# Storing the results of the mixture-of-experts units in order of the units, and gathering them by places that VectorE works out once per expert stage

## The reference, cut to what matters

```python
router_probs = jax.nn.softmax(flat @ router_w + router_b)
topk_probs, topk_idx = jax.lax.top_k(router_probs, 2)            # 2 of 8 experts for each of 4096 tokens
sh = jax.nn.gelu(flat @ sw1 + sb1); shared_out = sh @ sw2 + sb2  # 256 -> 512 -> 256, for every token
h1 = jax.nn.gelu(jnp.einsum('td,edh->teh', flat, rw1) + rb1)
expert_out = jnp.einsum('teh,ehd->ted', h1, rw2) + rb2
out = shared_out + sum of topk_probs * expert_out of the two chosen experts
```

## Time and profile before

| | |
|---|---|
| median of 3 runs | 4138.96 us (4134.91 to 4142.33) |
| the profiled execution, from its first to its last instruction (span) | 4122.5 us |
| median less span | 16.5 us |
| busy: PE, DVE, ACT, POOL | 3626.3, 2877.5, 1924.7, 1607.9 us |
| mean granted clock of PE | 0.951 of full speed |
| moved by DMA | 358.33 MB, of which 74.4 MB are the 142 clears of 512 KB |

### The profile page before, as it was taken

How to read it: one execution, slowest core, us unless ns; L and a number is a source line. 1 busy time by engine, 2 the same in 40 slices (tenths; PEclk the granted TensorE clock), 3 DMA queues, 4 the chain that set the end, 5 groups by cost and what they waited for, 6 DMA issues and landing times. The chain is left out here.

```text
span 4122.5 us, 60134 instructions
## 1 busy us (share of the span) xinstructions
PE 3626.3 (88%) x19193; PEld 2601.5 (63%) x19256; DVE 2877.5 (70%) x5355; ACT 1924.7 (47%) x4079; POOL 1607.9 (39%) x1485
## 2 busy tenths in 40 slices
PE   4888877999599999998799869887899799999998
PEld 3555556888588888887788735444666455554666
DVE  5777656656566666645665568886888666776898
ACT  3565644344355555544344344443344465666332
POOL 3766726444465666633644321101002444441000
PEclk8999978999899999999899989999999999999999
DMA  5999902465100000001356410001201444441000
GB/s 135 302 259 269 307 23 84 151 194 162 59 16 19 19 19 19 16 4 35 100 167 180 148 48 21 21 11 23 40 0 39 91 101 109 102 114 27 11 16 16
DMA packets 228873, 358.33 MB, mean 87 GB/s; under 512 B 36482, under 2 KB 132850, under 8 KB 221810
## 3 DMA queue, kind: packets, MB, share of 16 engines
q1 hardware_dynamic: 204038, 265.38, 22.1%
q0 software_dynamic: 24544, 89.36, 8.9%
HBM read 173.82 MB, written 172.20 MB: 84 GB/s over the span
## 5 line engine op out<-in xcount | busy, mean ns | idle before, releaser
L2894 DVE TENSOR_REDUCE ab_nmx<-banks 128x1 f32<-128x512 f32 x512 | 329.0, 684 | 136.0 <-PE banks L2681 133.8
L2825 ACT ACTIVATE ab_pt<-banks 128x512 f32<-128x512 f32 x512 | 283.0, 600 | 163.9 <-PE banks L2691 154.9
L1736 POOL TENSOR_TENSOR lb_pq<-lb_pq,lb_rr 128x512 f32<-128x512 f32 x192 | 206.2, 1077 | 305.1 <-DVE lb_rr L1597 301.8
L1462 ACT ACTIVATE lb_pq<-banks,lb_nmx 128x256 f32<-128x256 f32 x384 | 178.5, 470 | 229.4 <-DVE lb_nmx L1592 226.2
L2691 PE MATMUL banks<-ab_qT,ab_kT 128*128 128x512 f32 x512 | 252.3, 497 | 5.7 <-ACT ab_pt L2825 5.7
L358 ACT ACTIVATE da_pt<-banks 128x512 f32<-128x512 f32 (+1 forms) x384 | 179.3, 537 | 124.9 <-PE banks L270 120.6
L1592 DVE TENSOR_REDUCE lb_nmx<-banks 128x2 f32<-128x512 f32 x192 | 131.1, 683 | 148.0 <-PE banks L1314 146.8
L2681 PE MATMUL banks<-ab_kT,ab_qT 128*128 128x512 f32 x512 | 208.1, 410 | 21.1 <-DVE ab_nmx L2894 14.6
L285 PE MATMUL banks<-da_pt,da_vx 128*64 128x512 f32 (+3 forms) x1024 | 165.0, 467 | 35.3 <-POOL da_pt L578 31.8
L2465 PE MATMUL banks<-w_f_dT,f_hT 128*128 128x256 f32 x768 | 178.1, 382 | 4.0 <-ACT f_hT L2511 4.0
L576 POOL TENSOR_TENSOR da_pt<-da_pt,w_da_tri 128x384 f32<-128x384 f32 x128 | 148.0, 1157 | 85.7 <-ACT da_pt L358 85.6
(11 more groups left out here) (538 smaller groups left out, 11146.5 us busy)
## 6 DMA issues: line engine op xcount, KB each, us to landing
moe_xs<-zero SPq DMA_DIRECT2D x71, 512.0 KB, 11.8
moe_ys<-zero SPq DMA_DIRECT2D x71, 512.0 KB, 11.8
moe_a_w_raw<-in_moe_w SPq DMA_DIRECT2D x48, 512.0 KB, 3.9
moe_b_w_raw<-in_moe_w SPq DMA_DIRECT2D x48, 512.0 KB, 4.0
da_spill<-da_hi SPq DMA_DIRECT2D x128, 128.0 KB, 2.4
ab_spill<-ab_hi SPq DMA_DIRECT2D x128, 128.0 KB, 2.4
ab_qT<-ab_spill POOLq DMA_DIRECT2D x32, 392.0 KB, 5.7
ab_kT<-ab_spill POOLq DMA_DIRECT2D x32, 392.0 KB, 5.3
```

The source lines that it names most:

```text
L1462: nc.scalar.activation(pq[:, n % RING, t, :], ps[:, S_BANK + n % 2, 2 * P * t:2 * P * t + 2 * P], ACT.Exp, bias=nmx[:, n % RING, t:t + 1], ...
L1736: nc.gpsimd.tensor_tensor(pq[:, n % RING, :, :], pq[:, n % RING, :, :], bcast(rr[:, n % RING, :], 2, 2 * P), ALU.mult).then_inc(s_p, 1)
L2825: nc.scalar.activation(pt[:, s % RING, :], ps[:, EXP_BANK + s % 3, :], ACT.Exp, scale=AB_D ** -0.5).then_inc(s_e, 1)
L2894: nc.vector.tensor_reduce(nmx[:, g % 2, col:col + 1], ps[:, MAX_BANK + n % 3, :], op=ALU.max, axis=AX.X, negate=True).then_inc(s_mx, 1)
```

## The change

`store_y` writes unit u's result to rows 512u to 512u + 511 of `moe_ys`, a fixed address, and `moe_ys` shrinks to 23 x 512 = 11776 rows. It is no longer cleared: `clear_regions` runs over `moe_xs` alone (71 clears, 10 or 11 in a batch). The scatter still goes by `place` as before, and units still load their tokens and weights by the table. Since results now stand elsewhere than tokens, DVE rewrites `place` once per expert stage, in a new job `result_places` in step i = N - UNITS - 1 = 9, between `low_x(11)` and `take(9)`: to each place it adds, for the expert chosen, (first unit of the expert x 512 - its region). For that the places and the chosen experts are kept as floats for all batches in `Choice` (`placef`, `chosen_by`), and the counts and ends of the experts are worked out on 128 partitions, not one: the matmul of totals gives 128 rows, and `moe_fill` and `moe_upto` are loaded as broadcasts to 128 partitions.

```diff
@@ class Choice
+        self.placef = space.enter_context(core.nc.sbuf_tensor(f"{tag}_placef", [P, B, NT, TOPK], F32))
+        self.chosen_by = space.enter_context(core.nc.sbuf_tensor(f"{tag}_chosen_by", [P, B, NT, TOPK], F32))
@@ experts
-        count, ends, tablei = sb("count", [1, NE]), sb("ends", [1, NE]), sb("tablei", [1, 2, UNITS], U32)
+        count, ends, tablei = sb("count", [P, NE]), sb("ends", [P, NE]), sb("tablei", [1, 2, UNITS], U32)
...
+        taken = y[:, 0:2, :].rearrange("p t c -> p (t c)").rearrange("p (n e) -> p n e", e=NE)
@@ store_y
-                    sp.dma_start(rows_of(ys, entry(1, u, ROWS - UNIT)), y[:, :, :]).then_inc(s_stored[u % 2], 16)
+                    sp.dma_start(ys[u * UNIT:(u + 1) * UNIT, :].rearrange("(t p) c -> p t c", p=P),
+                                 y[:, :, :]).then_inc(s_stored[u % 2], 16)
@@ ranks
-                        nc.tensor.matmul(ps[0:1, ROUTE_BANK, 0:NE], w["moe_ones"][:, 0:1], before[:, NT, :],
+                        nc.tensor.matmul(ps[:, ROUTE_BANK, 0:NE], w["moe_ones"][:, :], before[:, NT, :],
@@ DVE, new job
+                def result_places():
+                    nc.vector.tensor_tensor(base[:, :], ends[:, :], count[:, :], ALU.subtract)
+                    dve.drain()
+                    nc.vector.scalar_tensor_tensor(base[:, :], base[:, :], float(UNIT), w["moe_region"][:, :],
+                                                   ALU.mult, ALU.subtract)
+                    experts_of = idf[:, :, :, :].rearrange("p b t k -> p (b t k)")
+                    rows = placef[:, :, :, :].rearrange("p b t k -> p (b t k)")
+                    nc.vector.tensor_tensor(taken[:, :, :], bcast(w["moe_iota"][:, :], 1, B * NT * TOPK),
+                                            bcast(experts_of, 2, NE), ALU.is_equal)
+                    dve.drain()
+                    nc.vector.tensor_tensor(taken[:, :, :], taken[:, :, :], bcast(base[:, :], 1, B * NT * TOPK), ALU.mult)
+                    dve.drain()
+                    nc.vector.reduce_sum(experts_of, taken[:, :, :], axis=AX.X)
+                    dve.drain()
+                    nc.vector.tensor_tensor(rows, rows, experts_of, ALU.add)
+                    dve.drain()
+                    for k in range(2):
+                        dve.wait_ge(s_scatter[k], per_batch * B // 2)
+                    nc.vector.tensor_copy(place[:, :, :, :].rearrange("p b t k -> p (b t k)"), rows)
+                    dve.drain()
@@ DVE, the loop over items
                     if i + 2 in number:
                         low_x(i + 2)
+                    if i == N - UNITS - 1:
+                        result_places()
                     if i in number:
                         take(i)
@@ network
-            ("moe_fill", a["moe_fill"]), ("moe_upto", a["moe_upto"]), ("moe_unit", a["moe_unit"])])
+            ("moe_fill", a["moe_fill"][0].partition_broadcast(P)), ("moe_upto", a["moe_upto"][0].partition_broadcast(P)),
+            ("moe_unit", a["moe_unit"])])
-        w["moe_ys"] = nc.dram_tensor("moe_ys", (ROWS, C), F32).ap()
+        w["moe_ys"] = nc.dram_tensor("moe_ys", (UNITS * UNIT, C), F32).ap()
@@ clear_regions
-            for k in range(part * 2 * blocks // parts, (part + 1) * 2 * blocks // parts):
-                rows = (w["moe_xs"], w["moe_ys"])[k // blocks][k % blocks * UNIT:(k % blocks + 1) * UNIT, :]
+            for k in range(part * blocks // parts, (part + 1) * blocks // parts):
+                rows = w["moe_xs"][k * UNIT:(k + 1) * UNIT, :]
```

More of the change, by code:

```diff
@@ L697, in experts @@
         top, idx = sb("top", [P, NT, 8]), sb("idx", [P, NT, 8], U32)
-        idf = sb("idf", [P, NT, TOPK])
-        tw, place = choice.tw, choice.place
+        tw, place, placef, idf = choice.tw, choice.place, choice.placef, choice.chosen_by
         oh = [sb(f"oh{k}", [P, NT, NE]) for k in range(TOPK)]
@@ L702, in experts @@
         b2 = sb("b2", [P, 2, C])
-        placef = sb("placef", [P, NT, TOPK])
+        base = sb("base", [P, NE])
         rank, spot = sb("rank", [P, NT, NE]), sb("spot", [P, TOPK, NT, NE])
-        count, ends, tablei = sb("count", [1, NE]), sb("ends", [1, NE]), sb("tablei", [1, 2, UNITS], U32)
+        count, ends, tablei = sb("count", [P, NE]), sb("ends", [P, NE]), sb("tablei", [1, 2, UNITS], U32)
         shift = sb("shift", [P, B, NT])
@@ L984, in weights @@
                     dve.drain()
-                    nc.vector.tensor_copy(idf[:, :, :], idx[:, :, 0:TOPK])
+                    nc.vector.tensor_copy(idf[:, b, :, :], idx[:, :, 0:TOPK])
                     dve.drain()
@@ L988, in weights @@
                         nc.vector.tensor_tensor(oh[k][:, :, :], bcast(w["moe_iota"][:, :], 1, NT),
-                                                bcast(idf[:, :, k], 2, NE), ALU.is_equal)
+                                                bcast(idf[:, b, :, k], 2, NE), ALU.is_equal)
                     dve.drain()
@@ L1008, in places @@
                     for k in range(TOPK):
-                        nc.vector.reduce_sum(placef[:, :, k], spot[:, k, :, :], axis=AX.X)
+                        nc.vector.reduce_sum(placef[:, b, :, k], spot[:, k, :, :], axis=AX.X)
                     dve.drain()
-                    nc.vector.tensor_copy(place[:, b, :, :], placef[:, :, :])
+                    nc.vector.tensor_copy(place[:, b, :, :], placef[:, b, :, :])
                     dve.drain().then_inc(s_place, 1)
@@ L1015, in units @@
                     dve.wait_ge(s_total, 1)
-                    nc.vector.tensor_copy(count[:, :], ps[0:1, ROUTE_BANK, 0:NE])
+                    nc.vector.tensor_copy(count[:, :], ps[:, ROUTE_BANK, 0:NE])
                     dve.drain()
                     nc.vector.tensor_tensor(parts_of[:, :, :], bcast(count[:, :], 2, NE),
-                                            bcast(w["moe_fill"][0:1, :], 1, NE), ALU.is_gt)
+                                            bcast(w["moe_fill"][:, :], 1, NE), ALU.is_gt)
                     dve.drain()
@@ L1022, in units @@
                     dve.drain()
-                    nc.vector.tensor_tensor(parts_of[:, :, :], bcast(count[:, :], 1, NE), w["moe_upto"][0:1, :, :], ALU.mult)
+                    nc.vector.tensor_tensor(parts_of[:, :, :], bcast(count[:, :], 1, NE), w["moe_upto"][:, :, :], ALU.mult)
                     dve.drain()
@@ L1026, in units @@
                     dve.drain()
-                    nc.vector.tensor_tensor(passed[:, :, :], bcast(w["moe_unit"][0:1, :], 2, NE), bcast(ends[:, :], 1, UNITS),
+                    nc.vector.tensor_tensor(passed[:, :, :], bcast(w["moe_unit"][0:1, :], 2, NE), bcast(ends[0:1, :], 1, UNITS),
                                             ALU.is_ge)
@@ L1031, in units @@
                     dve.drain()
-                    nc.vector.tensor_tensor(passed[:, :, :], passed[:, :, :], bcast(count[:, :], 1, UNITS), ALU.mult)
+                    nc.vector.tensor_tensor(passed[:, :, :], passed[:, :, :], bcast(count[0:1, :], 1, UNITS), ALU.mult)
                     dve.drain()
@@ L3270, in _ @@
             def _(sp):
-                sp.wait_ge(s_clear, 16 * 2 * ROWS // UNIT)
+                sp.wait_ge(s_clear, 16 * ROWS // UNIT)
         early.close()
```

2 lines of the change are left out of this document (1 added, 1 removed).

## The result

| | before | changed |
|---|---|---|
| median | 4136.24 us of 20 runs (4130.05 to 4146.87) | 4144.56 us of 20 runs (4134.63 to 4153.63) |
| ratio, 95% interval | 1 | 1.0018 (1.0010 to 1.0027) |
| the profiled execution, span | 4122.5 us | 4142.5 us |
| its own time | not known | 4144.66 us |

A repetition, with its own runs of the kernel before beside it, gave 1.0012 (1.0003 to 1.0022), 4140.1 against 4133.78 us. So the change costs 8.3 and 6.3 us, at or under the 8.3 us drawn ahead as the line of "no change", and both intervals lie above 1. The range (4130 to 4150) held and the call of "no change" too, the latter with nothing to spare in the first measurement; the sum behind them (+1.0 us) did not.

What follows compares the result with a forecast made beforehand. Bound: not DMA, but in the expert stages a unit loop through load_w2's landing. Terms 0 + 0.5 + 0.2 + 1.8 - 1.5 = +1.0 us gave span 4123.5, plus 16.5 around it 4140.0; range 4130 to 4150.

Steps and rivals of the forecast that it cites:

- Clears, 0: First stage: dropping 71 clears of 512 KB gains 0, hidden behind diff_attention's work; bounds -9 and 0.
- Two of its signs: In diff_attention: DMA share near a half in slices 2 to 5, and the stage's end within 2 us of before.
- Case C: Rival: the clears held the first stage, which loses up to 9 us, 4131, or 4005 if transfer-bound throughout; chance 0.13.
- Small tables, +0.5: Loads after batch 0's spills: 254 more short pieces may delay PE's first scores; +0.5 us, bounds 0 and +2.
- totals, +0.2: Expert counts on 128 partitions: a wider matmul and five DVE operations, with both stages together +0.2 us.
- The new places, +0.9 a stage: Seven DVE operations before take, 3.3 us, mostly covered by idle time; +1.8 us for both stages, bounds 0 and +6.
- two blockings of 2.4: Part of the upper bound for the new places: DVE held up twice by overlap with POOL, 2.4 us each.
- four small ones at 0.17: Four small DVE operations of the new places, 0.17 each at a pitch of 0.25, together 1.0 us.
- The last stores, -0.75 each: End of each expert stage: without the table read the last store goes out 0.75 us earlier; -1.5 us for two.
- The store near the second weights, taken as 0: Earlier units: store 2.4 us behind load_w2 instead of 3.1, taken as free; bounds 0 and +21 us.
- case B: Rival: in 42 units the earlier store delays the second weights' landing; 0.25 us a unit, +10.5, 4150.5; chance 0.16.
- A: The forecast's own case: everything is hidden or tiny; 4135 to 4146 us, predicted 4140.0; chance 0.68.

Runs made afterwards that it cites:

- x3: Changed kernel with 71 clears put back, of a spare table nobody reads: 4143.14 us, ratio 1.0026.
- x10: Changed kernel, places still early, with the second weights issued ahead of the first in SP's order: 4119.75 us, ratio 0.9964.
- x7: Kernel before with one edit, the second weights issued ahead of the first in SP's order: 4112.99 us, ratio 0.9949.
- x1: Changed kernel, but SP still reads the table ahead of each store and throws the value away: 4138.21 us, ratio 1.0024.
- x4: Kernel before plus only the places calculation into an unread tile, totals on 128 partitions and broadcast small tables: 4143.0 us, ratio 1.0020.
- n1: Kernel before, unchanged, run and profiled again: 4133.25 us, ratio 1.0001.
- x8: Changed kernel with places moved to the end of each expert stage and the table read kept ahead of the store, value unused: 4132.63 us, ratio 0.9995.
- x9: Changed kernel with its result store held back until the second weights have landed: 4135.84 us, ratio 1.0002.
- x2: Kernel before with only the store's address replaced by the fixed one, so gathers read other rows: 4139.0 us, ratio 1.0015.
- x5: Changed kernel with the places calculation moved to the end of each expert stage: 4138.51 us, ratio 1.0013.

## Why the prediction was right in its range and wrong in its sum

*Clears, 0: stood.* Waits for spills 17.6 us, head pairs 4.61, no wait of PE on a DMA. Two of its signs did not come, though neither tells against it: the share of DMA in slices 2 to 5 fell to 0.7 or 0.8 and not to a half, and the first logits came 4.2 us earlier in this pair of profiles, within the scatter that x3's paragraph gives. Case C did not come, and with it the Trainium skill's rule (SBUF — State Buffer, "A bandwidth-pool intuition that's wrong (but worth ruling out)") that HBM is almost always the bottleneck: 37 MB less written moved nothing that could be told. What a busy DMA line means is read from who waits.

*Small tables, +0.5, and totals, +0.2:* too small to see. The +0.43 of one pair of profiles lies within a scatter of 3 us.

*The new places, +0.9 a stage: the term was mis-sized.* Its bounds said at most 6 for both stages, but their own terms (0.6 and two blockings of 2.4, 5.4) are for one stage, so 10.8 for both. Early places give a mean of 113.7 us for the first four periods in five profiles, none or late ones 109.9 in five: +3.9 for both stages with the weights in their old order, and +7.4 (x10 less x7) with the second weights issued first. The step that failed is the sum of durations "four small ones at 0.17": I looked at POOL's first split only where `take` would meet it, not where my own last two operations would, though the earlier trace rows gave both POOL rows and a cast of 2.05. The large operations came through, as they began before POOL. What the early places do beyond these periods is open: in kernels with the store 3.0 to 3.1 us behind, later periods are 13.89 with early places (x1, x4) and 13.74 without (before, n1, x8).

The Trainium skill (SBUF — State Buffer, "Who interferes with whom") describes an exclusive lock: whichever starts first of a GpSimd operation that reads SBUF and a DVE operation with two SBUF inputs shuts the other out for its whole instruction; a cast can meet the same lock when it runs in a two-port mode. The trace agrees for both of ours: they began just behind POOL's operation and ended 0.06 to 0.09 us after it, with 64 columns. That the cast ran in such a mode no row shows. The Trainium skill also has it, in the same section, that a reduction never takes part on this chip; ours ended 0.06 us into POOL's operation, which tests nothing.

*The last stores, -0.75 each: right, at -0.70.* 0.08 us behind their rows for 0.78 before, and 0.62 in x8, where the read is back.

*The store near the second weights, taken as 0: this is the term that failed.* Eight stages with the store 2.4 us behind have a later period of 13.98 in the mean, ten with 3.0 to 3.1 have 13.80, the two of x9 13.81. The time from weights to cast is 4.96, 4.79 and 4.78. So 0.18 us a unit in the mean of all, 7.6 us over 42 units, where case B had 0.25 and 10.5. The mean hides that the nearness shows in the periods only where no places stand early: 14.06 near (x2, x5) for 13.74 (before, n1, x8), but 13.91 (after, x3) for 13.89 (x1, x4). How the cost divides in the changed kernel itself is therefore open. The reason given for 0, that the load of tokens stands between the two already, said nothing of what the store adds. Case B, with 0.16, was the likelier reading of my own rows: ACT waited for this landing almost every time, and a transfer moved nearer to it should not have been free. The groups overlap (x1's and x4's periods reach 13.95, x3's fall to 13.81), so it is the mean, x5 against x8, and x9 that carry this.

*The sum.* -1.4 + 3.9 + 7.6 is 10.1 us, against 8.3 and 6.3 in the medians. The 2 to 4 us between are open: they may be the clears (up to 4 us), or that the two costs overlap, as x1, x2, x4 and x5 suggest, each of which has one cost and 5 to 10 us. The stretch after moe_b alone, which no edit touches, differs by 12.5 us between profiles (1753.6 to 1766.1).

*The absolute number.* 4140.0 rests on 16.5 us around the span. It is 1.8 to 2.2 us, and the execution of before in the profile was quick by some 12 us. The step was to take a difference between two executions for a constant.

*What was luck.* The base was 2.7 us too high (4138.96, the median of three runs, for 4136.24 of twenty), which brought 4140.0 nearer to the measured 4144.56 than the sum earned: +1.0 was forecast and +8.3 measured. The range was wide enough for the case that partly came true, and A's own 4135 to 4146 holds the result although A's mechanism, everything hidden or tiny, did not hold. Of the signs, those of case B came: periods over 13.8 and longer waits of ACT for the second weights.

## What to carry to other kernels

A loop that runs through a transfer prices everything that comes near this transfer: find it, and multiply a tenth of a microsecond by its turns before you call an earlier store free; better, take the transfer out of the loop by its place in the queue, which gained 22 us (x7) where this change cost 6 to 8. Put small vector work where GpSimd rests, for its cost is set by what it runs beside and not by its size. And profile the kernel before twice, since the first profile here was 3.6 us quicker in one stage by chance alone.

## What the runs showed of the hardware that I had not expected

- An addition and a cast of 128x64 take 0.22 and 0.20 us with POOL at rest, 2.35 and 2.37 beside its split; the large operations ahead of them had ended, or all but ended, when POOL began. Which operation is caught shifts with a few tenths of a microsecond: of the two, both, one or none.
- A 512 KB load landed in 3.9 us when issued ahead of the other weights and 4.6 to 5.0 (medians of single profiles) when issued some 2 us behind them. A store 2.4 us behind it made its longest landing 6.0 to 6.6 us (after, x2, x3, x5). With the store 3.0 us or more behind, it was 5.2 to 5.6, with x1's 6.1 the exception.
- The read of an address from the table costs SP 0.7 us (0.78 less 0.08), and 0.54 where the value is thrown away (0.62 less 0.08, x1 and x8): more than the issue of the transfer that it is for (0.40).
